# First layer of a four-layer kernel: the squares of q and k as two float32r halves, and two products for each head mean

## The reference, cut to what matters

```
qkv = (xn @ Wqkv).reshape(B, N, 3, 16, 8)          # 16 heads of 8 features
q, k: rms_norm(z, scale) = scale * z / (|z| * 8 ** -0.5 + 1e-8)
attn = softmax((q @ k.T) * 8 ** -0.5)              # per head
x = x + (attn @ v) @ Wproj + bproj + experts(xn)
```

## Time and profile before

| | us |
|---|---|
| runs | 1885.95, 1890.72, 1898.35 (median 1890.72) |
| profiled execution | 1888.65, its span 1886.9, mean granted TensorE clock 0.947 |
| PE, DVE, ACT, POOL busy over the span | 1733.4, 1019.3, 830.8, 377.3 |
| the block `layer0_mix` | begins at 33.9 |

### The profile page before, as it was taken

The page is one execution under the profiler, slowest core; times in us unless marked ns, Lnnn a source line. Parts: engine busy times, 40 slices in busy tenths (PEclk is TensorE's granted clock), DMA queues, the critical chain, the costliest instruction groups (busy, mean ns, idle before and its releaser), DMA issues. The chain is left out here.

```text
span 1886.9 us, 22763 instructions
## 1 busy us (share of the span) xinstructions
PE 1733.4 (92%) x8614; PEld 1012.4 (54%) x8614; DVE 1019.3 (54%) x1660; ACT 830.8 (44%) x1018; POOL 377.3 (20%) x306
## 2 busy tenths in 40 slices
PE   7599999998887998999999999999999987999996
PEld 4122222222544445787878787777878753444443
DVE  3444454553675444454544545455545546877785
ACT  4367777784533334333333433433433343334332
POOL 1000000000455001202030302021111105444442
PEclk8689999999876999999999999999999998999998
DMA  1232222221101750000000000000000010000001
GB/s 73 32 62 46 46 46 46 46 46 58 60 1 36 174 146 5 1 1 1 1 1 2 1 1 1 1 1 1 1 1 1 1 55 0 1 0 1 0 1 45
DMA packets 19128, 49.12 MB, mean 26 GB/s; under 512 B 784, under 2 KB 1680, under 8 KB 18128
## 3 DMA queue, kind: packets, MB, share of 16 engines
q1 hardware_dynamic: 19024, 47.70, 10.8%
HBM read 45.21 MB, written 2.36 MB: 25 GB/s over the span
## 5 line engine op out<-in xcount | busy, mean ns | idle before, releaser
L494 ACT ACTIVATE probs<-ps_ring 128x1024 f32<-128x1024 f32 x256 | 246.1, 1023 | 126.8 <-PE ps_ring L708 123.9
L1765 PEld LDWEIGHTS ps_o<-v,probs 128*128 128x128 f32 x2048 | 235.3, 192 | 31.0 <-issue 25.6
L1765 PE MATMUL ps_o<-v,probs 128*128 128x129 f32 x2048 | 248.1, 278 | 1.7 <-ACT probs L1490 1.2
L1490 ACT ACTIVATE probs<-ps_ring 128x1024 f32<-128x1024 f32 x128 | 127.0, 1024 | 212.0 <-PE ps_ring L1746 212.0
L722 PE MATMUL ps_o<-probs,v 128*32 128x512 f32 x1024 | 141.8, 628 | 13.1 <-DVE o_sb L545 13.1
L1571 DVE TENSOR_REDUCE negmax<-ps_o 128x2 f32<-128x1024 f32 x64 | 78.5, 1226 | 137.1 <-PE ps_o L1721 137.1
L1483 ACT ACTIVATE xn<-ps_ring,pack 128x512 f32<-128x512 f32 x64 | 40.6, 685 | 162.7 <-PE ps_ring L1330 162.7
L1944 POOL TENSOR_TENSOR rs<-r,state 128x512 f32<-128x512 f32 x64 | 81.9, 1280 | 150.2 <-DVE state L2091 150.2
L1584 DVE RECIPROCAL rden<-ps_o 128x2 f32<-128x2 f32 x128 | 21.5, 168 | 144.0 <-PE ps_o L1765 144.0
L708 PEld LDWEIGHTS ps_ring<-q_stack,k_stack 32*128 32x128 f32 x512 | 31.9, 188 | 125.0 <-issue 104.6
L2091 DVE TENSOR_TENSOR_SCAN state<-decay,state,kv 128x511 f32<-128x511 f32 x64 | 91.6, 1431 | 6.5 <-issue 1.1
(11 more groups left out here) (371 smaller groups left out, 3501.9 us busy)
## 6 DMA issues: line engine op xcount, KB each, us to landing
cwb<-combine_by_expert SPq DMA_DIRECT2D x8, 2048.0 KB
score<-score_by_expert SPq DMA_DIRECT2D x7, 2048.0 KB, 13.7
pack<-pack_dram SPq DMA_DIRECT2D x1, 3840.0 KB, 14.9
pack<-pack_dram SPq DMA_DIRECT2D x1, 2507.0 KB, 8.5
x<-x_in SPq DMA_DIRECT2D x2, 1024.0 KB, 6.3
out<-x SPq DMA_DIRECT2D x1, 2048.0 KB, 6.3
score<-score_by_expert SPq DMA_DIRECT2D x1, 1536.0 KB, 13.6
pack<-pack_dram SPq DMA_DIRECT2D x1, 1451.0 KB, 6.1
```

Of the source, the lines that this page charges most:

```text
L494: nc.scalar.activation(probs[n % 3][:, 2 * half:2 * half + 2, :], ps, ACT.Exp, scale=float(HD0) ** -0.5).then_inc(read, 1)
L1490: nc.scalar.activation(probs[:, n % 2, m, :, :], ps, ACT.Exp).then_inc(read, 1)
L1765: last = nc.tensor.matmul(ps_o[:, i, k * (D + 1):(k + 1) * (D + 1)], probs[:, (b * PAIRS + p) % 2, m, j, queries], v[:, m, h, :], start=(m ...
```

## The change

`sq` is split like q and k are split already. On GpSimd each square of a batch is followed by a copy of `sq` into `sq_high`, which rounds to float32r, and by the subtraction `sq_low = sq - sq_high`; a drain stands behind each of the three, and the semaphore `squared` is raised by the subtraction. Before the copy GpSimd waits, in all batches but the first, until the head means of the batch before have been computed (`was_filled`). On VectorE, `mean_head` is copied once into a float32r tile `head_mean`, ahead of the copy of `select`. On TensorE each head mean is two float32r products added up in PSUM, in place of one float32 product; for batch 0 TensorE waits for `sel_ready` before them, where it waited for it behind them. 8.5 KB more of each partition is in use in this block.

```diff
+        sq_high, sq_low, head_mean = sb("sq_high", [P, 2, T]), sb("sq_low", [P, 2, T]), sb("head_mean0", [P, P])
...
+        def was_filled(eng, use):
+            n = turn_of[use]
+            eng.wait_ge(ring_done[n % RING0], n // RING0 + 1)
...
             for b in range(B):
                 was_read(pool, ("qk", b))
-                nc.gpsimd.tensor_tensor(sq[:, :, :], qk[:, :, :], qk[:, :, :], ALU.mult).then_inc(squared, 1)
+                nc.gpsimd.tensor_tensor(sq[:, :, :], qk[:, :, :], qk[:, :, :], ALU.mult)
+                pool.drain()
+                if b:
+                    was_filled(pool, ("ms", b - 1))
+                nc.gpsimd.tensor_copy(single(sq_high[:, :, :]), sq[:, :, :])
+                pool.drain()
+                nc.gpsimd.tensor_tensor(single(sq_low[:, :, :]), sq[:, :, :], sq_high[:, :, :], ALU.subtract).then_inc(squared, 1)
+                pool.drain()
...
             nc.vector.tensor_tensor(bound[:, 0:8], w["qs_row"], w["ks_row"], ALU.mult)
+            nc.vector.tensor_copy(single(head_mean[:, :]), sh["common"]["mean_head"])
             nc.vector.tensor_copy(single(sel[:, :, :]), w["select"].rearrange("p (s c) -> p s c", c=P)).then_inc(sel_ready, 1)
...
                 pe.wait_ge(squared, b + 1)
-                last = nc.tensor.matmul(ps[:, n, :], sh["common"]["mean_head"], sq[:, n, :], start=True, stop=True)
+                if b == 0:
+                    pe.wait_ge(sel_ready, 1)
+                for part, of in enumerate((sq_high, sq_low)):
+                    last = nc.tensor.matmul(ps[:, n, :], single(head_mean[:, :]), single(of[:, n, :]), start=(part == 0), stop=(part == 1))
```

## The result

22 runs of each kernel: 1896.04 us in the median after the change, 1889.62 before; the ratio is 1.0034, 95% interval 1.0023 to 1.0046, which is +4.3 to +8.7 us. One of the 22 runs after the change took 2190.3 us, at a granted clock of 0.732 where the others have 0.94; the ratio leaves it out. The profiled execution took 1894.83 us (span 1893.0, granted clock 0.943). TensorE is busy 5.4 us less, GpSimd 28 us more.

A forecast was written before the change was run, and what follows sets the result against it. TensorE was taken to set the pace from batch 1 on, with batch 0 a chain of waits. The terms -2.6 + 1.95 + 0 + 3.1 + 0.4 = +2.9 us on 1888.65 gave 1891.5 (own range 1887 to 1896), overall range 1884 to 1901.

The forecast's parts named there:

- (f): Rival in TensorE's head means: float32r from GpSimd leaves products as slow as before; +7.1 us, 1895.8, chance 0.01.
- (c): Rival on GpSimd: the copy is slow, upper ends in batch 0's chain and route; +9 us, 1897.7, chance 0.13.
- TensorE's products: Head means, seven batches: 0.9 us freed in each, only 0.37 counting because ScalarE is busier behind them; -2.6 us.
- GpSimd's operations: Behind the squares on GpSimd: copy 1.1 us, subtraction 2.0, drains about 0.2; squares ready 3.3 us later.
- L584's share: Batch 0's chain: this VectorE operation slips in before GpSimd's copy and adds 0.3 us.
- The chain's low end: Lower end of the forecast for batch 0's uncovered chain of head means: +1.0 us, beside +1.95 expected.
- The cover of 12.1 us: Later batches: time between squares' end and TensorE's head means, said to absorb GpSimd's added work; cost 0.
- Batch 0's chain: Batch 0's head means, uncovered: GpSimd's +3.3 and +0.3, less 1.65 for faster products; +1.95 us.
- The cast of `mean_head`: VectorE's first casts: the new copy takes over a memset wait and the cast of select stands again; +0.4 us.
- `route`: VectorE's batch 0 routing: GpSimd's copy and subtraction for batch 1 block its comparisons while TensorE waits; +3.1 us.
- Rival (b): In route, VectorE's short comparisons keep their place and GpSimd's copy waits; -0.25 us, 1888.4, chance 0.15.
- Rival (d): TensorE's granted clock falls otherwise as batch 0's pauses change length; 1886 to 1897, chance 0.14.

The follow-up runs named there:

- e1: Changed kernel with TensorE's side only: GpSimd squares once into float32r, both products read that tile, no copy or subtraction; 0.9986 of before, -2.6 us.
- e2: As e1, but one float32r product for each head mean instead of two; 0.9969 of the kernel before, -5.9 us.
- e6: Kernel before plus two unused reciprocals at the end of VectorE's part of the block, a 3.6 us delay; 1.0028 of before, +5.3 us.
- e9: Kernel before plus two unused reciprocals on VectorE ahead of route's comparisons, a 3.6 us delay; 1.0011 of before, +2.1 us.
- e12: Kernel before with ScalarE's four rms steps at s = 7, 8, 10, 11 instead of 7 to 10; 0.9976 of before, -4.5 us.
- e8: Changed kernel again, unchanged, for a second profile; 1.0036 of the kernel before, +6.8 us.
- e4: Changed kernel, but for batch 1 GpSimd's copy waits until VectorE's route is done; 1.0006 of the kernel before, +1.1 us.
- e3: Kernel before plus GpSimd's side only: copy and subtraction done and waited for, TensorE keeps the float32 product; 1.0053 of before, +10.0 us.
- e7: Kernel before again, unchanged, for a second profile; 0.9997 of the kernel before.
- e5: Changed kernel, but VectorE squares batch 0 for a float32 product; batch 1's copy waits for route, mean_head cast behind route; 0.9994 of before, -1.1 us.
- e11: As e5, with ScalarE's four rms steps at s = 7, 8, 10, 11 instead of 7 to 10; 0.9950 of the kernel before, 1883.21 us.

## Why the prediction was right in sign and half in size

The range (1884 to 1901) held, and so did "within 1%". The forecast, +2.9 us, lies below the interval of +4.3 to +8.7, and the measured 1896.04 just above the narrower range of 1887 to 1896 that it was given. 1.0 us of the distance from 1891.5 is the starting point: one execution of 1888.65, where the median turned out 1889.62. By the total alone rivals (f), 1895.8, and (c), 1897.7, were nearer; the timeline rules both out, with products of 0.4 us at the full clock and a copy of 1.04 to 1.35 us.

- **TensorE's products, the term that was furthest off.** Durations were right (four take 1.19 to 1.22 us at the full clock, 2.07 at the half). That most of the 0.9 us freed is lost was right: e1 and e2 show that TensorE does not limit behind them. The size was 0.27 us a batch, not 0.37: 0.13 us of the pause counted from the earlier trace rows remains (200.18 to 200.31), as exponentials in that stretch start about that much behind an rms step. Seven times: -1.9, not -2.6. The stretch behind the turned weights is shorter by 0.9 only: a mean of 379.2 us in six profiles with the means in float32r, 380.1 in six without. The upper level is slightly more frequent there (21 of 30 beside 18 of 30), but each group spreads over 2 to 3 us (377.5 to 380.5, 378.7 to 380.9), so that this 0.9 is itself uncertain by more than a microsecond.
- **GpSimd's operations.** Copy 1.04 to 1.35 us (1.1 forecast), subtraction 2.34 to 2.47 (2.0). The squares are ready 3.7 us later; 3.6 was forecast with L584's share, so a subtraction 0.35 too cheap and a share 0.23 too dear nearly cancel, which is luck. The chain's low end should have been 3.0 - 1.65 = +1.35, not +1.0. The cover of 12.1 us held. The Trainium skill calls one-input work on GpSimd roughly line-rate ("GPSIMD Engine Reference", section 4.1); the trace bears it out, with 1.04 us for the copy where nothing stood in its way, beside the 0.9 estimated from it.
- **Batch 0's chain, the second term that failed.** I priced it against 3.55 us for the old products, read from one execution. Against that execution it is right (12.79 - 10.51 = +2.3, 2.35 forecast, and the first rms step at 46.88 where 46.8 was forecast), but other profiles of the same code have the products at 1.98. The mean from memset to first rms step over the kernel before and its like (10.51, 9.17, e6 10.36, e9 9.17, e12 10.30) is 9.90; over after, e8 and e4 (12.79, 12.99, 13.23) 13.0. So +3.1, not +1.95 + 0.4; how often each clock occurs in the timed runs is not known.
- **The cast of `mean_head`.** It and the cast of `select` went side by side behind the memset: 1.78 us from memset to L518, 1.71 before. 0.1, not 0.4.
- **`route`.** +2.98 against 3.1, in every kernel with GpSimd's full chain beside it (after, e3, e8), gone in e4. Rival (b) did not happen: one comparison slipped in between GpSimd's operations and no more. The trace agrees with what the Trainium skill says of an exclusive lock ("SBUF — State Buffer", "SBUF: two separate sides"), which is held for a whole instruction and counts for operations of VectorE with two inputs in SBUF beside a GpSimd operation that reads it: three comparisons stood, the longest 2.4 us in all, while e9's reciprocals, with one input, took their 1.75.
- **Sum with measured terms.** 3.1 + 3.0 - 0.9 = +5.2; the block totals give 431.0 - 426.0 = +5.0 (after and e8; before, e7 and e6). Of the 2.3 us between this and the forecast 1.7 are TensorE's term and 0.75 batch 0's chain. The other 1.2 to 1.4 of 6.4 lie within the interval; whether they are spread or come from the stretches behind the block stays open. Those strayed by 10 us from profile to profile, 1425.8 to 1435.8, with and without the change; they were longest in profiles with a mean clock of 0.937 to 0.942 (e4, e3, e12) and shortest in those with 0.946 and 0.947 (before, e5, e11).
- **Rival (d)** was there in part: in batch 0's head means the kernel before and its like had the full clock in two of five profiles, the changed one in none of three.

## What to carry to other kernels

Work given to GpSimd is not free where VectorE has operations with two inputs in SBUF beside it: here one comparison stood beside each GpSimd operation until that was over, and since TensorE was waiting for VectorE, `route` was 3.0 us longer; let such work wait until the VectorE stretch is through (e4). Before freeing an engine that is 94% busy, ask stage by stage who is waited for there: two kernels with 0.9 and 1.4 us freed a batch gained the same 0.27, while moving ScalarE's steps apart, with no engine relieved, gave -4.5 us (e12), though which stretch gains it is not shown. And a short stretch priced from one profile may stand at either clock; take the same stretch from a second one.

## What was not expected of the hardware

Batch distances fell on two levels 1.57 us apart, by whether the clock stood at 0.76 or 1.00 in the mean over the batch's start. Six profiles without float32r means have three upper distances of five each, though not for the same batches. Batch 0's head means ran at either clock: at 2.4 GHz in e1, e7, e9 and e11 (pauses of 1.2 to 1.6 us in front of them), at 1.2 GHz in all others (1.85 to 6.5 us). Before and e7 are the same kernel, and between them that alone is worth 1.5 us of a chain without cover. Why the clock was up in one and down in the other is not shown. VectorE's reciprocal ran at its usual 1.75 us beside GpSimd's squares, where a two-input comparison of 32 elements took 1.9.
